# Layer 0's token stage moved into its attention: each group's tokens are normalised, split, turned and scored two groups later

## The reference

```
x = x + _L0_gnn_ref(_layernorm(x), adj, W, a)
tokens = _layernorm(x)
logits = tokens @ router_w.T            # top 2 of softmax, weights renormalised
out = tokens + sum_e combine[:, e] * (gelu(tokens @ w1[e] + b1[e]) @ w2[e] + b2[e])
x = x + out
```

## Time and profile before

| what | us |
|---|---|
| timed runs, median of 3 | 1396.8 |
| timed runs, lowest and highest | 1385.87 and 1396.86 |
| profiled execution, span | 1413.2 |
| TensorE busy | 1090.2 (77%) |
| VectorE busy | 963.9 (68%) |
| GpSimd busy | 696.6 (49%) |
| ScalarE busy | 550.3 (39%) |

### The profile page before, as it was taken

One profiled execution on the slowest core, in us unless ns is written; L12 is line 12 of the kernel. 1 busy time (PEld: TensorE's weight loads), 2 busy tenths in 40 slices (PEclk: granted clock), 3 DMA queues, 4 the chain that ended last, 5 costly groups with the idle time before them and its releaser, 6 DMA issues.

```text
span 1413.2 us, 31628 instructions
## 1 busy us (share of the span) xinstructions
PE 1090.2 (77%) x9392; PEld 894.5 (63%) x9393; DVE 963.9 (68%) x1851; ACT 550.3 (39%) x1229; POOL 696.6 (49%) x752
## 2 busy tenths in 40 slices
PE   6999482479999962556776486489999997799995
PEld 4777372468888852345564372377879886587774
DVE  4889688847777742568897888656666654466664
ACT  3666486422222211556776575022222222122221
POOL 3577681155555527546670380142533125776652
PEclk9999755589999995888889659599999998899998
DMA  9211151045555543234452553555767433443430
GB/s 283 55 46 39 60 179 60 13 120 158 160 157 158 163 131 102 71 83 139 117 158 59 162 181 104 47 168 163 209 178 177 138 110 113 128 129 119 122 111 12
DMA packets 126095, 172.53 MB, mean 122 GB/s; under 512 B 35109, under 2 KB 94000, under 8 KB 125744
## 3 DMA queue, kind: packets, MB, share of 16 engines
q0 software_dynamic: 28288, 83.03, 21.4%
q1 hardware_dynamic: 89504, 88.22, 19.9%
q10 hardware_dynamic: 8208, 0.07, 0.9%
HBM read 100.87 MB, written 71.44 MB: 122 GB/s over the span
## 4 chain that ended last, share of the span: by engine, by line
PE 52%; issue 19%; DVE 10%; POOL 5%; ACT 5%; another core or an unknown queue 4%; DMA 2%; SPq 1%; DVEq 1%; POOLq 0%; ACTq 0%
PE bank L964 20%; PE bank L978 18%; PE bank L782 5%; PE bank L947 4%; POOL arena L649 2%; ACT b_bc L1037 1%; PE bank L810 1%; DVE X L1279 1%; DVE arena L1623 1%; DVE stats L1269 1%; PE bank L900 1%; PE bank L800 1%; DMA stage_w<-in_L_ffn_W 1%; DVE arena L1624 1%
## 5 line engine op out<-in xcount | busy, mean ns | idle before, releaser
L1187 ACT ACTIVATE arena<-bank,b1T 128x256 f32<-128x256 f32 (+1 forms) x464 | 176.0, 457 | 565.2 <-PE bank L964 360.7
L964 PE MATMUL bank<-arena,WREG 128*128 128x256 f16 (+1 forms) x2784 | 323.8, 268 | 20.5 <-issue 17.9
L978 PE MATMUL bank<-WREG,arena 128*128 x2544 | 309.4, 275 | 35.8 <-issue 32.0
L978 PEld LDWEIGHTS bank<-WREG,arena 128*128 128x128 f16 x2544 | 247.1, 99 | 80.5 <-issue 48.8
L964 PEld LDWEIGHTS bank<-arena,WREG 128*128 x2784 | 253.0, 99 | 61.0 <-issue 31.6
L1693 DVE CAST arena<-arena 128x1024 f16<-128x1024 f32 (+1 forms) x140 | 83.9, 599 | 193.2 <-ACT arena L1187 154.8
L668 POOL DMA_INDIRECT arena<-split_tokens,gather_row x136 | 130.6, 960 | 148.7 <-PE bank L947 59.5
L782 PE MATMUL bank<-wg_sb,arena 128*128 128x258 f32 x512 | 142.9, 426 | 45.4 <-ACT arena L1010 29.0
L597 POOL DMA_INDIRECT WREG<-expert_outputs,pos_both x128 | 126.9, 991 | 99.4 <-PE bank L769 38.8
L679 POOL DMA_INDIRECT X<-token_rows,gather_row x72 | 73.5, 1021 | 176.0 <-DMA first_rows<-X 83.4
L782 PEld LDWEIGHTS bank<-wg_sb,arena 128*128 128x128 f32 x512 | 103.7, 212 | 71.8 <-ACT arena L1010 33.9
(11 more groups left out here) (204 smaller groups left out, 1528.7 us busy)
## 6 DMA issues: line engine op xcount, KB each, us to landing
first_rows<-X SPq DMA_DIRECT2D x72, 257.0 KB, 4.6
expert_outputs<-arena SPq DMA_DIRECT2D x68, 256.0 KB
X<-in_x SPq DMA_DIRECT2D x16, 512.0 KB, 6.0
split_tokens<-arena SPq DMA_DIRECT2D x16, 512.0 KB, 2.9
stage_w<-in_L_ffn_W SPq DMA_DIRECT2D x16, 512.0 KB
token_rows<-X SPq DMA_DIRECT2D x8, 1024.0 KB
...
```

The lines of the kernel that those rows point to most:

```text
L964: last = mm(hb, w1_at(L, ea, wh, kc, fc), tT[:, tb:tb + width], start=n == 0, stop=n == 3 * KC - 1)
L978: last = mm(ob[a], hsrc[:, h0:h0 + P], w2_at(L, e[a % len(e)], wh, fc), start=fc == 0 and n == 0, stop=fc == FC - 1 and n == 2)
L1187: ins = A(hid[:, h0:h0 + width], bank[2 + 2 * (u % 2) + fc // 2][:, b0:b0 + width], ACT.Gelu if L == 0 else ACT.Relu, bias=cut(b1T, ea * F ...
```

## The change

The statistics, 1/std, normalising, splitting, turning and scoring of group g - 2 are done inside iteration g of the attention, for g = 2 to 7; those of groups 6 and 7 follow the loop. Buffers for it (a ring of four pairs and two turned pairs) lie in the upper half of the weights' region. first_norm becomes norms(k), which handles group k for the attention and group k - 3 for the tokens together; inverse_root(k) does the same on GpSimd and also forms -mean/std, in place of the square root on ScalarE and the column-wide reduction. GpSimd now casts to f16 (high_tokens) and VectorE subtracts (low_tokens). Turned pairs with even numbers are copied by VectorE, those with odd numbers by ScalarE. The turned tokens share banks 0 and 1 with the turned x. The logits go to bank 5, in two halves of 16 pairs; the turned probabilities move from bank 5 to bank 4. SP's stores stand between its loads of adjacency and weights. The last two weight splits stand behind all of this. Layer 1 is as before, and the old token stage is kept for it.

The core of the diff:

```diff
+        ring_y32 = [ring0[:, 512 * k:512 * (k + 1)] for k in range(4)]
+        ring_y16 = ring0[:, 2048:4096].bitcast(F16)
+        ring_yT = [ring0[:, 4096 + 512 * k:4608 + 512 * k].bitcast(F16) for k in range(2)]
+        lg_both, lg_low = ring0[:, 5120:5632], ring0[:, 5632:5888]
...
+        def turned_copied(eng, p):
+
+            eng.wait_ge((yT_act if p % 2 else yT_ev)[0], at(p // 2 + 1))
...
+        def blocks_of(a, groups):
+
+            by_group = a.rearrange("p (g t) -> p g t", t=GT)
+            return by_group[:, groups[0]:groups[-1] + 1:3, :]
+
+        def norm_groups(k):
+
+            return [g for g in (k - 3, k) if 0 <= g < GROUPS]
...
+                def store_tokens(k):
+
+                    sp.wait_ge(yl_ready[0], at(2 * k + 2))
+                    sp.dma_start(table.rearrange("(t p) c -> p t c", p=P)[:, 4 * k:4 * k + 4, :],
+                                 ring_y16[:, k % 2 * 2048:(k % 2 + 1) * 2048].rearrange("p (t c) -> p t c", t=4)).then_inc(y_stored[k % 4][0], 16)
...
+                        if g >= 2:
+                            store_tokens(2 * (g - 2))
                         for k in range(2):
                             load_weights(g, k)
+                        if g >= 2:
+                            store_tokens(2 * (g - 2) + 1)
...
+            def inverse_root(k):
+
+                groups = norm_groups(k)
+                v, r, u = (blocks_of(col[n], groups) for n in ("var", "rstd", "ta"))
+                pool.wait_ge(var_ready[0], at(k + 1))
+                second = k >= 3
+                for turn in range(3):
                     step(nc.gpsimd.tensor_tensor(u, r, r, ALU.mult))
                     step(nc.gpsimd.tensor_tensor(u, u, v, ALU.mult))
                     step(nc.gpsimd.tensor_scalar(u, u, -0.5, 1.5, ALU.mult, ALU.add))
                     ins = nc.gpsimd.tensor_tensor(r, r, u, ALU.mult)
-                    if k < 2:
+                    if turn < 2 or second:
                         step(ins)
-                    else:
-                        ins.then_inc(pool_rstd[0], 1)
+                if second:
+                    m, a, r = (one(n, groups[0] * GT, GT) for n in ("nm2", "mean", "rstd"))
+                    ins = nc.gpsimd.tensor_tensor(m, a, r, ALU.mult)
+                ins.then_inc(pool_rstd[0], 1)
+
+            def high_tokens(p):
+
+                pool.wait_ge(y_ready[0], at(p + 1))
+                pool.wait_ge(yT_mm[0], at(p - 3))
+                if p % 2 == 0 and p >= 4:
+                    k = p // 2 - 2
+                    pool.wait_ge(y_stored[k % 4][0], 32 + 16 * (k // 4))
+                y16_t = ring_y16.rearrange("p (t c) -> p t c", c=2 * D)[:, 2 * (p % 4):2 * (p % 4) + 2, 0:D]
+                nc.gpsimd.tensor_copy(y16_t, ring_y32[p % 4].rearrange("p (t d) -> p t d", d=D)).then_inc(hi_ready[0], 1)
...
+                        inverse_root(g + 1)
                         if g + 1 < GROUPS:
                             no_edges(g + 1)
+                        p = 4 * (g - 2)
+                        if g >= 2:
+                            high_tokens(p)
+                            high_tokens(p + 1)
                         cut_weights(g - 1, 0)
+                        if g >= 2:
+                            high_tokens(p + 2)
                         cut_weights(g - 1, 1)
+                        if g >= 2:
+                            high_tokens(p + 3)
+                    for g in range(GROUPS - 2, GROUPS):
+                        inverse_root(g + 3)
+                        for p in range(4 * g, 4 * g + 4):
+                            high_tokens(p)
                     cut_weights(GROUPS - 1, 0)
...
+                if L == 0 and n >= 4 and q < 2:
+                    turned_copied(pe, 4 * (n - 4) + 2 + q)
...
+            def turn_pair(p):
+
+                pe.wait_ge(yl_ready[0], at(p + 1))
+                if p >= 2:
+                    turned_copied(pe, p - 2)
+                if p // 4 + 3 < GROUPS and p % 4 < 2:
+                    pe.wait_ge(xT_ev[0], at(4 * (p // 4 + 3) + p % 4 + 3))
+                for j in range(8):
+                    last = nc.tensor.transpose(bank[p % 2][:, j * (P // 2):(j + 1) * (P // 2)].bitcast(F16),
+                                               ring_y16[:, (8 * (p % 4) + j) * P:(8 * (p % 4) + j + 1) * P], ident16[:])
+                last.then_inc(yT_mm[0], 1)
+
+            def logits_of(p):
+
+                turned_copied(pe, p)
+                if p == TILES // 4:
+                    pe.wait_ge(half_ready[0], at(1))
+                for a in range(2):
+                    for yh, kc in ((0, 0), (1, 0), (1, 1), (0, 1)):
+                        n = E if yh else 2 * E
+                        b = (4 * a + yh * KC + kc) * P
+                        last = mm(cut(bank[5], (2 * p + a) % (TILES // 2) * 2 * E, n), ring_yT[p % 2][:, b:b + P],
+                                  rt16[:, kc * 2 * E:kc * 2 * E + n], start=(yh, kc) == (0, 0), stop=(yh, kc) == (0, 1))
+                last.then_inc(logit_mm[0], 1)
...
+                    if tokens and g > 2:
+                        logits_of(p - 1)
+                    if n < GROUPS:
                         project(L, n, 1)
                         turn_x(L, n, 3)
                     turn_probs(L, g)
                     if n < GROUPS:
                         project(L, n, 2)
+                    if tokens:
+                        turn_pair(p)
                     attend(L, g, 0)
                     if n < GROUPS:
                         project(L, n, 3)
+                    if tokens:
+                        turn_pair(p + 1)
+                        logits_of(p)
                     attend(L, g, 1)
+                    if tokens:
+                        turn_pair(p + 2)
+                        logits_of(p + 1)
                     attend(L, g, 2)
                     if n < GROUPS:
                         edges(L, n)
+                    if tokens:
+                        logits_of(p + 2)
                     attend(L, g, 3)
+                    if tokens:
+                        turn_pair(p + 3)
+                if L == 0:
+                    for p in range(4 * (GROUPS - 2), TILES // 2):
+                        turn_pair(p)
+                        logits_of(p - 1)
+                    logits_of(TILES // 2 - 1)
 
                 def turn_tokens(i, q):
                     pe.wait_ge(yl_ready[L], at(i * 8 + q + 1))
...
+            def normal_tokens(p):
+
+                act.wait_ge(pool_rstd[0], at(p // 4 + 4))
+                act.wait_ge(yl_ready[0], at(p - 3))
+                for a in range(2):
+                    t = 2 * p + a
+                    ins = A(ring_y32[p % 4][:, a * D:(a + 1) * D], xs(t), ACT.Identity, scale=one("rstd", t), bias=one("nm2", t))
+                ins.then_inc(y_ready[0], 1)
+
+            def copy_turned(p):
+
+                act.wait_ge(yT_mm[0], at(p + 1))
+                act.wait_ge(logit_mm[0], at(p - 1))
+                A(ring_yT[p % 2], bank[p % 2][:].bitcast(F16), ACT.Copy).then_inc(yT_act[0], 1)
...
                         copy_xT(L, n, 2)
+                    if tokens:
+                        normal_tokens(p)
+                    if n < GROUPS:
                         scale_rows(L, n, 2)
                         scale_rows(L, n, 3)
                         copy_xT(L, n, 3)
+                    if tokens:
+                        normal_tokens(p + 1)
                     copy_probs(L, g)
                     if n < GROUPS:
                         scale_rows(L, n, 4)
                         scale_rows(L, n, 5)
+                    if tokens:
+                        normal_tokens(p + 2)
                     exp_of_rows(L, g, 0)
                     if n < GROUPS:
                         scale_rows(L, n, 6)
                         scale_rows(L, n, 7)
+                    if tokens:
+                        copy_turned(p + 1)
                     exp_of_rows(L, g, 1)
+                    if tokens:
+                        normal_tokens(p + 3)
                     if n < GROUPS and L == 1:
                         diagonal(L, n)
                     ahead = L == 1 and g + 2 < GROUPS
...
+                    if tokens:
+                        copy_turned(p + 3)
+                if L == 0:
+                    for p in range(4 * (GROUPS - 2), TILES // 2):
+                        normal_tokens(p)
+                        if p % 2 and p > 4 * (GROUPS - 2) + 1:
+                            copy_turned(p - 2)
+                    copy_turned(TILES // 2 - 1)
+                else:
+                    act.wait_ge(var_ready[L], at(1))
+                    A(col["sd"], col["var"], ACT.Sqrt, bias=eps_col[:]).then_inc(sd_ready[L], 1)
+                    act.wait_ge(rs2_ready[L], at(1))
 
                 def normalise(i, q):
...
+            def norms(k):
+
+                ch.wait()
+                groups = norm_groups(k)
```

(60 more changed lines are left out.)

159 lines of the change are left out of this document (78 added, 81 removed).

## The result

The changed kernel has a median of 1401.7 us (20 runs, 1393.9 to 1411.3), the kernel before 1393.6 in the same series (20 runs, 1385.9 to 1402.4): a ratio of 1.0068, 95% interval 1.0049 to 1.0087. The forecast was 1.7 us less; measured are 8.1 us more between the medians, 9.5 by the ratio. That is inside the 1% which I took for what a measurement can tell from no change, but the interval is 0.4% wide and lies above 1: it is clearly a loss, and the reason lies in what I priced.

What follows compares the result with a forecast made beforehand. The attention was taken as bound by a loop of links between engines, not one full engine. Attention +33.9 and tail with joining -35.6 gave -1.7, so 1396.8 became 1395.1 us; eight times in ten, 1383 to 1408.

Steps and rivals of the forecast that it cites:

- The chain: Layer 0's attention loop: in-order links between engines set 23.0 us per group instead of 17.1; chance 0.52.
- steps from P: Six links of one attention group, timed from P, the start of project(n, 0), to the next P at 23.0 us.
- rival of pure load (B): Attention: new steps slip into waits, so load alone gives 20.4 us per group, in all 1380; chance 0.18.
- Rival E: Token stage does not shrink because pairs of groups 6 and 7 wait: tail 35 instead of 21, 1409; chance 0.04.
- the tail: From the attention's last write to X to the joined logits: 20.9 us where it was 56.2, saving 35.3.
- rival (C): Attention: TensorE's stalls lower its clock to 0.91, +2.5 per group, in all 1410; decides below 0.98; chance 0.16.
- the forecast's 21.4: Attention's last interval, into group 7: 21.4 us instead of 23.0, as no turn of x follows group 7.
- the same chain without projection: Group 7, from its probabilities to the last write of X: 16.6 us where it took 12.1, +4.5.
- The port pair (D): Attention: VectorE adds and subtractions wait out GpSimd's 1.49 us, +0.7 to +1.5 per group, 1402; chance 0.10.

Runs made afterwards that it cites:

- a1: Changed kernel with GpSimd's fourth cast of a group, high_tokens(p+3), moved behind the next group's diagonal; ratio 1.0046 to the kernel before.
- after: The changed kernel itself, against the kernel before; median 1401.7 us, ratio 1.0068.
- a2: Changed kernel with logits_of(p) moved behind attend(g, 1) on TensorE; ratio 1.0036 to the kernel before.
- a3: Changed kernel with turn_pair(p+3) ahead of attend(g, 3) and ScalarE's copy_turned(p+3) ahead of the last exponential; ratio 1.0093 to the kernel before.
- b1: Changed kernel with all weight splits and their loads moved behind the stage; single run for its trace, stage 166.2 us against 167.3.
- b3: Changed kernel with the last group's second_stats and norms ahead of low_tokens(24) and (25) on VectorE; ratio 1.0051 to the kernel before.
- a4: Changed kernel with the moves of a1, a2 and a3 together; ratio 1.0011 to the kernel before.
- c2: a4 with b3's order in the tail and VectorE's copy_turned(p+2) given to ScalarE; ratio 1.0001 to the kernel before.
- d3: Changed kernel with the moves of a4 and b3 together; ratio 0.9953 to the kernel before.

## Why the prediction was wrong

**The chain was right.** Point by point for the group above, against the steps from P: end of attend 0 9.2 us (forecast 9.7), copy of VectorE 12.7 (12.75), exponential 14.8 (14.8), diagonal 17.9 (17.65), attend 3 21.1 (20.75), next P 23.3 (23.0). The rival of pure load (B), at 20.4, is refuted for this kernel: its loop never ran below 23.3, and no variant with the pairs and the splits in it below 22.5. Rival E, too: the tail shrank as worked out.

**The step that failed is the price of TensorE's work behind a stall.** In the forecast a stall had the price of its own length and the products behind it that of the full clock; the clock was a rival (C) that decides below 0.98. It was 0.93 or 0.96 in three of five groups, so C came in part: 1.7 us for a group with slow products (25.01 against 23.33), where C had 2.5 in each. The error over the five intervals is +5.8 us (119.5 for 113.7), and a1, which has the full clock throughout, saves 5.6 of them. That the two agree is luck. a1 also takes a link out, 0.67 us per group, which the forecast had priced (0.65). Laid out by interval, the error is:

- the three usual ones, 71.7 for 69.0: 1.0 is the chain, 23.33 instead of 23.0, and 1.7 the clock;
- the first, 23.95 for 23.0, which is 23.66 in a1 at the full clock too;
- the last, 23.87 for 21.7 (the forecast's 21.4, carried over to the soft maxima): at the full clock a1 has 22.23 there, only 0.4 less than its period, where I had taken off 1.6 because group 7 is followed by no turn of x. By a1 and its link some 1.2 us of the 2.2 are this term, and the other 1.0 the clock (an estimate from these rows).

So the clock is some 2.7 us of the 5.8, and the rest are sizes of the chain. Why a stall is followed by the lower level in one group and not in the next stays open: after 22 waits of 2.2 to 2.5 us at `edges` (after, a2, a3, b1, b3) the two products took over 1.5 us twelve times, after eleven waits of 1.84 or 1.85 (a4, c2, d3) twice, after five of 0.76 or 0.87 (a1, after) never.

**The second is group 7.** I gave it "the same chain without projection", 16.6 us from its probabilities to the last write of X. It took 20.2 (188.33 to 208.48). Three attends at 2.02, 2.05 and 1.83 instead of 1.02 are 2.8 more, two turns ahead of them at 1.03 and 1.06 instead of 0.61 another 0.9. And the add at 196.00, beside GpSimd's last split step, took 1.64 instead of 0.69, with TensorE's wait of 3.00 behind it: 0.95. That is more than the error of +3.6, so other terms of the 16.6 were too long. The earlier trace rows had the token stage at 0.57 of the clock, and I used half-clock prices in the tail, but not here, though the kernel before was already at 0.71 in its group 7.

**The third is the tail,** 22.2 for 20.9: ScalarE could start the last four pairs 12.55 us after the last write (221.03 - 208.48), 11.9 forecast, and the rest took 9.7 instead of 9.0. The order behind it was seen rightly: without the two subtractions ahead of the statistics (b3) the tail is 1.9 shorter.

**The port pair (D)** is right as a mechanism and was wrong as a price. Beside GpSimd's tensor-tensor instructions VectorE waits until these end: the add of group 7 ends at 197.64, 0.55 us behind the split step (195.94 + 1.15 = 197.09), and the third of the norms' small instructions, normally 0.16, takes 1.03 beside the diagonal in every group.

```profile
131.34 1.03 DVE L1448 TENSOR_TENSOR cols<-stats 128x8 f32<-128x8 f32 x1
```

It ends at 132.37, the diagonal (131.24 + 1.10) at 132.34. Beside the mask of 1.49 us an add lost only 0.35 to 0.38 again, and ended before it. The Trainium skill, "SBUF — State Buffer", section on the two separate sides, says that the later of the two engines blocks for the whole instruction; the trace agrees for the diagonal and the subtraction of the splits, and not for the mask. In the loop most of these stretches are off the chain and cost nothing there. One isn't, the add ahead of VectorE's copy, which D had named: b1 shows it at 0.36 us per group, about the 0.3 by which the chain was short. D had 0.7 to 1.5.

**The balance.** Outside, a pair costs 50.2 / 32 = 1.57 us, at half clock. Inside it costs 35.2 / 20 = 1.76 in the five intervals and 8.15 / 4 = 2.0 in group 7; with the three links shortened, at the full clock, (22.55 - 17.07) / 4 = 1.37. So a pair in the attention isn't hidden, it is merely done elsewhere, at nearly the same price, and what isn't moved keeps a latency of 22 us. The forecast had 23.0 - 17.1 = 5.9 per group, 1.48 per pair, just under 1.57; an error of 0.3 per pair turned a small gain into a small loss.
